# Softmax exponentials taken by head on ScalarE, gate-times-up products moved to VectorE, one epsilon moved to GpSimd, and the last stage put in another order

## What is computed

```python
q = rmsnorm(q, gq)                       # 16 heads of 128
k = rmsnorm(k, gk)                       # 64 keys a batch
scores = einsum('bqhd,bkhd->bhqk', q, k) * scale
attn = softmax(scores, axis=-1)
out = einsum('bhqk,bkhd->bqhd', attn, v) ... @ Wo
x = _layernorm(x + out)
qx, sx, sc = _reorder_quantize_x(xf, up_reorder_index)
g = _qlinear(qx, sx, sc, w_gate, ...)
u = _qlinear(qx, sx, sc, w_up, ...)
t = silu(g) * u                          # 704 hidden features
qt, st, sct = _reorder_quantize_x(t, down_reorder_index)
y = _qlinear(qt, st, sct, w_down, ...)
x = _layernorm(x + y)
```

## Time and profile before

| | |
|---|---|
| median of 3 runs | 630.56 us (630.09 to 634.25) |
| profiled execution, its own time | 634.27 us |
| its span, first to last instruction | 632.5 us |
| mean granted TensorE clock | 0.988 |
| PE / DVE / ACT / POOL busy | 93% / 74% / 61% / 48% of the span |

### The profile page before, as it was taken

How to read it: one execution, slowest core, us unless ns; L and a number is a source line. 1 busy time by engine, 2 the same in 40 slices (tenths; PEclk the granted TensorE clock), 3 DMA queues, 4 the chain that set the end, 5 groups by cost and what they waited for, 6 DMA issues and landing times.

```text
span 632.5 us, 11059 instructions
## 1 busy us (share of the span) xinstructions
PE 588.6 (93%) x3696; PEld 445.2 (70%) x3696; DVE 467.8 (74%) x786; ACT 387.0 (61%) x881; POOL 301.6 (48%) x244
## 2 busy tenths in 40 slices
PE   6999779989899999999999999999999999999873
PEld 3653579988898888597788778779854655555631
DVE  5979999999999985544544552563536699899996
ACT  4579899999999956623222222231555577758642
POOL 7023589999999993123333333353222231515110
PEclk9999799999999999999999999999999999999988
DMA  8001561211211108244432432351410000000100
GB/s 286 1 2 36 142 243 52 67 51 57 61 51 58 43 2 308 91 188 171 171 107 98 171 112 92 123 183 62 151 59 0 1 2 0 2 0 2 34 1 33
DMA packets 18434, 52.43 MB, mean 83 GB/s; under 512 B 3873, under 2 KB 9648, under 8 KB 16721
## 3 DMA queue, kind: packets, MB, share of 16 engines
q1 hardware_dynamic: 15344, 42.36, 19.2%
q0 software_dynamic: 2752, 7.34, 3.9%
q10 hardware_dynamic: 288, 2.10, 0.9%
HBM read 47.13 MB, written 4.67 MB: 82 GB/s over the span
## 4 chain that ended last, share of the span: by engine, by line
PE 63%; DVE 16%; ACT 13%; issue 5%; DMA 2%; POOL 0%; DVEq 0%; POOLq 0%; ACTq 0%
PE ps L2189 11%; ACT arena L703 7%; PE ps L2267 6%; PE ps L2197 6%; ACT arena L718 3%; PE ps L1972 3%; PE ps L1957 3%; PE ps L2251 3%; PE ps L1806 3%; PE ps L2217 2%; PE ps L2006 2%; PE ps L2129 2%; PE ps L1815 2%; PE ps L1959 2%; DVE arena L1320 2%
## 5 line engine op out<-in xcount | busy, mean ns | idle before, releaser
L473 POOL TENSOR_TENSOR arena<-arena 128x1024 f32<-128x1024 f32 x63 | 147.3, 2378 | 4.1 <-DVE arena L1320 3.8
L1320 DVE TENSOR_TENSOR_SCAN arena<-arena,ps 128x1024 f32<-128x1024 f32 x64 | 143.4, 2279 | 4.8 <-ACT arena L703 1.3
L703 ACT ACTIVATE arena<-arena,a_neg 128x510 f32<-128x510 f32 x128 | 84.8, 713 | 1.9 <-DVE arena L1320 1.7
L2189 PEld LDWEIGHTS ps<-arena 128*128 128x128 f32 x660 | 75.5, 192 | 3.9 <-issue 3.1
L2189 PE MATMUL ps<-arena 128*128 128x128 f32 x660 | 77.4, 277 | 0.1
L1957 PE MATMUL ps<-ident,arena 128*128 128x128 f32 x384 | 65.0, 279 | 10.0 <-ACT arena L714 9.0
L1972 PE MATMUL ps<-ident,arena 128*128 128x128 f32 x512 | 67.3, 273 | 2.6 <-DVE arena L1329 1.8
L914 ACT ACTIVATE arena<-ps 128x256 f32<-128x256 f32 x45 | 17.3, 384 | 82.5 <-PE ps L2189 82.5
L718 ACT ACTIVATE arena<-arena,b_tok 128x512 f32<-128x512 f32 x96 | 65.0, 712 | 0.0
L1972 PEld LDWEIGHTS ps<-ident,arena 128*128 128x128 f32 x512 | 57.8, 141 | 4.0 <-DVE arena L1329 1.3
L2267 PE MATMUL ps<-arena 128*128 128x512 f32 x128 | 59.2, 596 | 1.6 <-ACT arena L942 1.2
(11 more groups left out here) (315 smaller groups left out, 1150.5 us busy)
## 6 DMA issues: line engine op xcount, KB each, us to landing
arena<-in_w_moe SPq DMA_DIRECT2D x8, 2176.0 KB, 9.0
arena<-c_dram SPq DMA_DIRECT2D x32, 256.0 KB, 3.2
arena<-in_w_o ACTq DMA_DIRECT2D x1, 2048.0 KB, 12.8
arena<-in_w_qT SPq DMA_DIRECT2D x1, 2048.0 KB, 9.9
arena<-in_w_q SPq DMA_DIRECT2D x1, 2048.0 KB, 8.0
arena<-moe_out SPq DMA_DIRECT2D x8, 256.0 KB, 4.6
x<-in_x SPq DMA_DIRECT2D x2, 512.0 KB, 4.6
arena<-in_w_in SPq DMA_DIRECT2D x2, 512.0 KB, 5.3
```

What stands on the lines that cost most here:

```text
L473: pool.tensor_tensor(in_chunks(hC[unit % 3]), in_chunks(h[unit % 3]), c_bc[:, m % C_BUFS, :].unsqueeze(1).to_broadcast([P, 2, HALF]), ALU. ...
L703: ins = nc.scalar.activation(dA_b[:, unit % 2, 2 * k:2 * k + 2, 1:], dt_b[:, c, 2 * half:2 * half + 2, 1:], ACT.Exp, scale=a_neg[:, c, n:n ...
L1320: nc.vector.tensor_tensor_scan(h[unit % 3], dA[:, k, :], ps[:, 2 * k:2 * k + 2, :].rearrange("p a b -> p (a b)"), 0.0, ALU.mult, ALU.add). ...
L2189: ins = nc.tensor.matmul(ps[:, bank, c * P:(c + 1) * P], w13[:, k, chunk * P:(chunk + 1) * P], xT[:, k, :], start=(k == 0), stop=(k == KD ...
```

## The change

1. `BY_HEAD` names all eight tiles. For them `take_scores` only takes the maximum. `scale_scores` works on 16 columns: it makes `below_top` = -maximum x rstd. `exponential` is 16 instructions of 128x64, one for each head, which read the scores from PSUM, with `q_rs` as scale, `below_top` as bias (each a column with one value a partition), and the sum of the head in `total_e` by the accumulator. `softmax` no longer sums. The two score banks are free only when the exponentials are done (`s_exp` in place of `s_taken`).
2. `query_rstd` on GpSimd adds the epsilon itself; VectorE's `add_epsilon` is gone.
3. `product` of all eight tiles is on VectorE; `prod`, `t_in`, `t_size` and `tinv` have two buffers.
4. The lists of all four engines are in another order. Some waits go with it: the first queries wait for one part of `x1T`, not two, the banks of the second half of `query_keys` are dealt out anew, and `normalise_early` comes last on ScalarE.

```diff
+        BY_HEAD = range(0, TILES)
+        scores = ps[:, 2:4, :].rearrange("p a (h t) -> p (a h) t", t=KV)
...
             def query_rstd(t):
+                pool.wait_ge(s["q_squared"], 4 * t + 4)
+                pool.tensor_scalar(q_ms[:, t % 2, :], q_ms[:, t % 2, :], 1e-5, None, ALU.add).then_inc(s["q_eps"], 1)
                 pool.wait_ge(s["q_eps"], t + 1)
-                if t >= 2:
+                if t - 2 in BY_HEAD:
+                    pool.wait_ge(s["s_exp"], t - 1)
+                elif t >= 2:
                     pool.wait_ge(s["s_shifted"], t - 1)
...
             def exponential(t):
                 act.wait_ge(s["s_shifted"], t + 1)
+                if t in BY_HEAD:
+                    if t >= 2:
+                        act.wait_ge(s["s_soft"], t - 1)
+                    for hd in range(HEADS):
+                        ins = nc.scalar.activation(shift[:, t % 2, hd, :], scores[:, hd, :], ACT.Exp, bias=below_top[:, t % 2, hd:hd + 1],
+                                                   scale=q_rs[:, t % 2, hd:hd + 1], accum_out=total_e[:, t % 2, hd:hd + 1])
+                    ins.then_inc(s["s_exp"], 1)
+                    return
...
                 link(nc.vector.tensor_reduce(top[:, t % 2, :], scores, axis=AX.X, op=ALU.max))
-                nc.vector.tensor_tensor(shift[:, t % 2, :, :], scores, over(top, t), ALU.subtract).then_inc(s["s_taken"], 1)
+                if t not in BY_HEAD:
+                    nc.vector.tensor_tensor(shift[:, t % 2, :, :], scores, over(top, t), ALU.subtract).then_inc(s["s_taken"], 1)
 
             def scale_scores(t):
+                dve.wait_ge(s["q_rstd"], t + 1)
+                if t in BY_HEAD:
+                    nc.vector.scalar_tensor_tensor(below_top[:, t % 2, :], top[:, t % 2, :], -1.0, q_rs[:, t % 2, :], ALU.mult, ALU.mult).then_inc(s["s_shifted"], 1)
+                    return
...
-                link(nc.vector.tensor_reduce(total_e[:, t % 2, :], shift[:, t % 2, :, :], axis=AX.X, op=ALU.add))
+                if t not in BY_HEAD:
+                    link(nc.vector.tensor_reduce(total_e[:, t % 2, :], shift[:, t % 2, :, :], axis=AX.X, op=ALU.add))
...
             def bank_free(users, mine, n=1):
                 for name in users:
-                    if issued[name]:
+                    if name == "s_taken" and issued[name] - 1 in BY_HEAD:
+                        pe.wait_ge(s["s_exp"], issued[name])
+                    elif issued[name]:
                         pe.wait_ge(s[name], issued[name])
...
-                    if 4 * t + g == 0:
-                        pe.wait_ge(s["x1T_done"], 2)
```

More of the change, by code:

```diff
@@ L1546, in _ @@
             over = lambda v, t: v[:, t % 2, :].unsqueeze(2).to_broadcast([P, HEADS, KV])
-            scores = ps[:, 2:4, :].rearrange("p a (h t) -> p (a h) t", t=KV)
             def take_scores(t):
@@ L1674, in _ @@
             scale_of_tokens(0)
+            take_scores(2)
+            scale_scores(2)
             round_tokens(0)
-            add_epsilon(2)
             add_attention(1)
-            scale_scores(2)
+            scale_of_tokens(1)
+            softmax(2)
+            round_tokens(1)
             take_gate(0)
             take_up(0)
-            softmax(2)
-            scale_of_tokens(1)
+            take_gate(1)
+            product(0)
             scale_of_hidden(0)
-            round_tokens(1)
@@ L1685, in _ @@
             take_scores(3)
+            scale_scores(3)
+            take_up(1)
             round_hidden(0)
-            add_epsilon(3)
-            take_gate(1)
-            take_up(1)
-            scale_scores(3)
+            product(1)
             add_attention(2)
+            softmax(3)
+            scale_of_tokens(2)
             scale_of_hidden(1)
-            scale_of_tokens(2)
             add_result(0)
             round_tokens(2)
+            take_scores(4)
+            scale_scores(4)
@@ L1712, in _ @@
             scale_scores(5)
+            round_tokens(3)
             add_attention(4)
+            scale_of_tokens(4)
+            softmax(5)
+            product(2)
+            round_tokens(4)
+            take_scores(6)
+            scale_scores(6)
+            scale_of_hidden(2)
+            softmax(6)
             take_gate(3)
+            add_attention(5)
+            round_hidden(2)
+            scale_of_tokens(5)
             take_up(3)
-            scale_of_tokens(4)
-            add_result(2)
@@ L1736, in _ @@
[L1736 to L1748 removed]
+            take_gate(4)
+            product(3)
+            add_result(1)
+            scale_of_hidden(3)
+            round_tokens(5)
@@ new lines, in _ @@
+            take_scores(7)
+            take_up(4)
+            scale_scores(7)
+            round_hidden(3)
+            product(4)
+            add_attention(6)
+            scale_of_hidden(4)
+            add_result(2)
+            softmax(7)
+            round_hidden(4)
+            scale_of_tokens(6)
+            add_result(3)
+            take_gate(5)
+            add_result(4)
+            take_up(5)
+            round_tokens(6)
+            product(5)
+            scale_of_hidden(5)
+            add_attention(7)
```

342 lines of the change are left out of this document (151 added, 191 removed).

## The result

The changed kernel takes 646.75 us (median of 4, 646.13 to 650.43) against 630.33 of the kernel before: a ratio of 1.0255, 95% interval 1.0227 to 1.0283, 16 us slower. The forecast was 636.6, its range 626 to 644.

The account below looks back on a forecast made before the run. TensorE was taken to set the pace while queries remain, then VectorE's list the end. VectorE's end 5.6 us later plus 0.4 for the output made + 6.0 on the median 630.56: 636.6 us, range 626 to 644.

Parts of the forecast that it names:

- waits at scores(1) 1.5 ...: 8.7 us: TensorE up to gate(3): eight waits, at scores, values, queries and gates, for ScalarE's exponentials or squares, 8.7 us in all.
- The part on GpSimd: GpSimd's query power: adding the epsilon takes its own 0.3 us, on an engine that waits most of the stage.
- The earlier first queries gain nothing: TensorE at the stage's start: moving the first queries ahead brings no gain, since scores(1) waits after the same work.
- what would make the forecast too fast: Sign on TensorE: a granted clock below 1 in the waits would make the predicted time too short; no size given.
- the price of a head: ScalarE's exponentials by head: 0.37 us a head, 6.0 us a tile of 16 heads.
- both rivals on it: ScalarE's exponentials: columns hidden, 0.28 us a head, 628.5 us, chance 0.26; or costlier, 0.41 a head, 642, chance 0.12.
- The rival of hidden columns: ScalarE's exponentials: scale and bias fetched during accumulator reads, 0.28 us a head, end 8.1 us earlier at 628.5; chance 0.26.
- TensorE's work: TensorE from the stage's start at 446.08 us to gate(3): 121.2 us of work without the waits.
- the tail: VectorE's list from the softmax of tile 6 to its end: 57.4 us, against 48.4 before.
- the harm of GpSimd's epsilon at 0: VectorE beside GpSimd's epsilon: no slowdown, priced at 0; the port lock rule would give up to 2.4 us.
- VectorE's relief of some 26 us: VectorE: 31 us off from softmax steps, 5.3 us on from six products; net some 26 us, and the blocked steps.
- The relief wins: Rival at VectorE's list behind the softmax of tile 6: TensorE not held, end 4.4 us earlier or more, 623.2; chance 0.10.

Follow-up runs that it names:

- e10: e1 with the exponentials by head without scale and bias columns, which alters the output; 627.71 us, ratio 0.9943.
- e1: The changed kernel with GpSimd's memset of the padding moved from ahead of to behind the first query power; 642.18 us, ratio 1.0170.
- e8: e1 with two products that nobody reads put on TensorE ahead of scores(6); 640.86 us, ratio 1.0138.
- e14: e1 with the exponentials by head taking a scale column but no bias, the maximum still worked out and waited for; 629.28 us, ratio 0.9974.
- e6: The kernel before with only the epsilon moved from VectorE to GpSimd, ahead of each query power; 630.78 us, ratio 0.9995.
- e3: The changed kernel with BY_HEAD empty: one exponential instruction a tile, subtraction, scaling and sum on VectorE again; 641.25 us, ratio 1.0154.
- e9: The changed kernel with both the memset behind the first query power and BY_HEAD empty (e1 and e3 together); 633.79 us, ratio 1.0037.
- e2: The changed kernel with VectorE's normalise_results(2) ahead of scale_scores(0), the memset left in place; 647.56 us, ratio 1.0269.
- e4: The changed kernel with four products that nobody reads put on TensorE ahead of scores(6); 646.41 us, ratio 1.0236.

## Why the prediction was wrong

- **Failed: "waits at scores(1) 1.5 ...: 8.7 us", TensorE's waits up to gate(3).** With the slower products behind them they came to 18.5 (139.9 less the 121.4 of work of e10). 5.3 of them are the memset (e1). The part on GpSimd looked at that engine's own 0.3 us and at its idle time; it didn't look at what stood in its queue ahead of the first power, nor what that waited for once four steps of keys times weights had been moved behind the first scores. "The earlier first queries gain nothing: by scores(1) TensorE has done the same work as before, and waits" is right about the work; the wait it speaks of was 1.75 us without the memset in the way (e1), and with it 4.59 us, two steps earlier.
- **Mis-sized, the same term:** the remaining waits are 13.1 us. The gaps, 9.9, are near the list. The lower clock after the 1.95 us ahead of scores(6) was named as what would make the forecast too fast, and left out of the sum: 1.8 us, of which filling the gap gave back 0.9 (e8). The edges of the gaps, 1.5, were not in it either.
- **Right: the price of a head** (0.38 against 0.37), so that both rivals on it fall. Columns are not hidden, and a head doesn't cost 0.41. The rival of hidden columns had its point of decision well placed (0.30 us a head) and its gain too small: 8.1 us, where e14 at 0.29 gained 12.4.
- **Right: TensorE's work** (121.2; 121.4 in e10), **the tail** (57.4; 58.0), and the harm of GpSimd's epsilon at 0 (e6). The output's late 512 KB cost nothing, where 0.4 was taken.
- **Right, and of use only in part:** VectorE's relief of some 26 us. VectorE is idle for 23.2 us in front of the softmaxes; what lies behind the softmax of tile 6 counts, as the sum had it (the tail is 61.6 us with the old exponentials, e3, and 58.0 now).
- **The relief wins** falls. Even with TensorE nearly free of waits, at a head of 0.20 or 0.29 us and the memset out of the way (e10, e14), the time is 3.6 and 1.6 us below the kernel before by the ratios, where the rival began at 4.4.

What stays open is why no more comes of the new order by itself. With the old exponentials (e9) the softmax of tile 6 begins 123.5 us behind the stage's start, 9.8 earlier than before (133.3), but VectorE's tail grows by 13.4 (61.9 against 48.4), and the run is 2.3 us behind. Which moves in the lists would shorten that tail was not tried. Nor was the share of the held banks in the 8.4 us separated from that of ScalarE's queue.

## What to carry to other kernels

When an order is changed, read for each moved step every wait that counts it, on engines that the change doesn't touch too: a 0.15 us memset cost 5 us because its wait had been free only in the old order. Before work is moved to an engine with room, ask what that engine then holds: here ScalarE had the time, but it held two PSUM banks that TensorE wanted, and mean squares stood behind it; and the first pointer column fitted into TensorE's cover where the second didn't. The largest idle row need not be the one that costs; swapping the two calls at it (e2) moved the wait and changed nothing.

## What was not expected of the hardware

The exponential of 64 columns out of PSUM with its accumulator's read takes 0.20, 0.29 and 0.38 us start to start with no, one and two columns of scale and bias: each column adds 0.09, and the read of the accumulator covers none of it. TensorE's granted clock fell behind two gaps of the changed kernel, of 4.59 us and of 1.96 us; the windows from the end of the first on:

```profile
470.00:474.00 4.00, 1.42 (x5) 1.25 (x6) 0.82 (x3) 2.08 (x11) 1.59 (x1) 0.60 0.00 0
474.00:478.00 4.00, 4.00 (x6) 1.54 (x5) 0.00 (x0) 4.00 (x22) 0.00 (x0) 0.55 0.00 0
478.00:482.00 4.00, 4.00 (x11) 1.72 (x10) 2.12 (x4) 4.00 (x22) 0.00 (x0) 1.00 0.02 4
```

It is near the lower of its levels, 1.2 GHz, when TensorE is busy again, and back at 2.4 from 478; behind the gaps of 1.50 and 1.62 us of this kernel the granted clock stayed at 1.00 (513 to 517, 535 to 540 us). Products whose result nobody reads kept it at 1.00 in the second place (e4).
